# A new step order for a fused decoder: queries projected between the two halves of the weighing

## The reference

```python
for i in range(DEPTH):                                   # 6 layers
    x = attn_layer(shift_tokens(x), Wqkv[i], q_scale[i], k_scale[i], Wo[i]) + x
    x = ffn_layer(shift_tokens(x), ln_g[i], ln_b[i], W1[i], b1[i], W2[i], b2[i]) + x

def attn_layer(x, Wqkv, qs, ksc, Wo):                    # 16 heads of 64
    q, k, v = split(x @ Wqkv)                            # 128 -> 3 * 1024
    q = l2norm(q) * qs;  k = l2norm(k) * ksc
    q, k = rotary(q, k)                                  # x*cos + rotate_half(x)*sin, scaled
    sim = einsum(q, k_of_own_and_previous_window) * 8    # windows of 32, masked
    out = softmax(sim) @ v
    return out @ Wo                                      # 1024 -> 128

def ffn_layer(x, g, bln, W1, b1, W2, b2):
    xn = layernorm(x) * g + bln
    a, gate = split(xn @ W1 + b1)                        # 341 hidden, twice
    return a * gelu(gate) @ W2 + b2
```

## Time and profile before

| | |
|---|---|
| median of three runs | 2215.07 us |
| profiled execution, its own time | 2222.9 us |
| span of its trace | 2221.1 us |
| PE busy | 2012.4 us (91%) |
| DVE busy | 1410.5 us (64%) |
| ACT busy | 1384.2 us (62%) |
| POOL busy | 1090.0 us (49%) |
| mean granted TensorE clock | 0.983 of full speed |

### The profile page before, as it was taken

How to read it: one execution, slowest core, us unless ns; L and a number is a source line. 1 busy time by engine, 2 the same in 40 slices (tenths; PEclk the granted TensorE clock), 3 DMA queues, 4 the chain that set the end, 5 groups by cost and what they waited for, 6 DMA issues and landing times.

```text
span 2221.1 us, 74774 instructions
## 1 busy us (share of the span) xinstructions
PE 2012.4 (91%) x32616; PEld 1183.0 (53%) x32616; DVE 1410.5 (64%) x1975; ACT 1384.2 (62%) x2029; POOL 1090.0 (49%) x709
## 2 busy tenths in 40 slices
PE   8999997789998999999999999999899998999987
PEld 5655654355555555555555555555555555555553
DVE  1454444667766776676667667766677676667753
ACT  5555554466666666766666666666666666666664
POOL 0000000576665665565656656665556555556540
PEclk9999998799999999999999999999999999999998
DMA  3000000122223222232222323222322223222220
GB/s 106 1 1 1 1 20 29 39 59 59 59 68 78 68 69 59 64 93 62 68 62 68 85 58 84 61 58 69 78 69 69 59 59 88 67 69 59 60 59 20
DMA packets 82066, 128.11 MB, mean 58 GB/s; under 512 B 17230, under 2 KB 28108, under 8 KB 81740
## 3 DMA queue, kind: packets, MB, share of 16 engines
q1 hardware_dynamic: 81740, 123.33, 21.4%
HBM read 21.55 MB, written 1.05 MB: 10 GB/s over the span
## 4 chain that ended last, share of the span: by engine, by line
PE 66%; ACT 13%; issue 11%; DVE 7%; POOL 2%; DMA 0%; ACTq 0%; POOLq 0%; DVEq 0%; SPq 0%
PE ps L617 11%; PE ps L613 11%; PE ps L639 8%; PE ps L677 7%; PE ps L670 6%; PE ps L697 4%; PE ps L426 3%; PE ps L622 3%; DVE work L1104 2%; PE ps L626 2%; ACT work L974 2%; POOL work L1421 2%; ACT work L981 2%; DVE work L1252 2%; PE ps L519 1%
## 5 line engine op out<-in xcount | busy, mean ns | idle before, releaser
L1421 POOL TENSOR_TENSOR work<-work,RS 128x1024 f32<-128x1024 f32 x192 | 365.6, 1904 | 345.8 <-ACT RS L961 342.0
L617 PEld LDWEIGHTS ps<-ident,work 128*128 128x128 f32 x3072 | 344.4, 141 | 254.5 <-issue 112.9
L617 PE MATMUL ps<-ident,work 128*128 128x128 f32 x3072 | 408.7, 276 | 68.4 <-ACT work L981 32.0
L1099 DVE TENSOR_TENSOR work<-ps,work 128x512 f32<-128x512 f32 (+1 forms) x288 | 244.6, 849 | 253.7 <-ACT work L1019 182.5
L1442 POOL TENSOR_TENSOR work<-work 128x1024 f32<-128x1024 f32 x96 | 225.8, 2352 | 149.1 <-DVE work L1104 148.9
L1427 POOL TENSOR_TENSOR work<-work,RL 128x1024 f32<-128x1024 f32 x96 | 182.8, 1904 | 141.8 <-DVE RL L1159 141.8
L1432 POOL TENSOR_TENSOR work<-work 128x1024 f32<-128x1024 f32 x96 | 226.8, 2362 | 51.0 <-DVE work L1104 51.0
L1104 DVE TENSOR_TENSOR work<-ps,work 128x512 f32<-128x512 f32 (+1 forms) x288 | 246.9, 857 | 0.0
L1144 DVE TENSOR_REDUCE SS<-work 128x16 f32<-128x1024 f32 x192 | 231.9, 1208 | 0.0
L677 PEld LDWEIGHTS ps<-work 64*32 64x32 f32 x12288 | 136.2, 105 | 166.9 <-issue 153.8
L670 PEld LDWEIGHTS ps<-KT,work 64*32 64x32 f32 x12288 | 136.6, 105 | 127.5 <-issue 125.7
(11 more groups left out here) (184 smaller groups left out, 3177.9 us busy)
## 6 DMA issues: line engine op xcount, KB each, us to landing
work<-work SPq DMA_DIRECT2D x576, 128.0 KB
work<-work SPq DMA_DIRECT2D x336, 64.0 KB
WQ<-in_wqkv SPq DMA_DIRECT2D x6, 512.0 KB, 3.6
WK<-in_wqkv SPq DMA_DIRECT2D x6, 512.0 KB, 4.1
WV<-in_wqkv SPq DMA_DIRECT2D x6, 512.0 KB, 3.5
WO<-in_wo SPq DMA_DIRECT2D x6, 512.0 KB, 3.9
work<-ZR SPq DMA_DIRECT2D x48, 64.0 KB
W<-in_w SPq DMA_DIRECT2D x6, 341.0 KB, 3.0
```

The costliest lines, as they stand in the source:

```text
L617: m = nc.tensor.transpose(flat(R)[:, t * 128:t * 128 + 128], src[:, t * 128:t * 128 + 128], ident[:, :])
L1099: V.tensor_tensor(h16(cos_part[:, j, cols]), h16(src), rotary_tabs[:, at:at + 64].unsqueeze(1).broadcast_to([PARTS, heads_in, 64]), ALU.mu ...
L1421: U.tensor_tensor(h16(qk_norm[:, j, :]), h16(cos_part[:, j, :]), inv_norms[:, j, :].unsqueeze(2).broadcast_to([PARTS, 16, 64]), ALU.mult). ...
```

## The change

The same instructions are kept, and the order within a step is new on TensorE, ScalarE, VectorE and GpSimd; SyncE is the same.

- TensorE: the query projection of block g+1 now stands between `weigh(0, 4)` and `weigh(4, 8)` of step g (`queries`). The values come first in a step, then the turned heads, then the FFN or output piece, then the keys' turn. `variance` comes right behind the scores. In the second block's step the hidden chunks 0, 1 and 2 stand around the turns of the keys and the queries, and two thirds of `ffn_project` come before the weighing; its last third is in n = 2.
- ScalarE: `copy_heads` moves from the end of a step to the next one, behind the square of the queries. Exp of the scores moves from the start of the next step to the end of its own, ahead of `invert_norms(g, 1)`. In the second block's step the values are copied before the turned heads, the GELU table is loaded behind `copy_heads`, and the GELUs stand among the copies.
- VectorE: row sum and reciprocal move to the end of their own step; `norm` comes ahead of `sums(1)`; the three `gated` stand around the sin product and `sums(0)`.
- GpSimd: the order of the second block's `norm_product` is as in the other steps.

```diff
+            def queries(g):
+                pe.wait_ge(block_shifted, 2 * (g + 1))
+                pe.wait_ge(wq_loaded, 16 * (g // 16 + 1))
+                project(bank_z, w_q, 0, g % 4)
+                project(bank_z, w_q, 1, g % 4).then_inc(q_projected, 1)
...
-                if a:
...
-                    project(bank_z, w_q, 0, n)
-                    project(bank_z, w_q, 1, n).then_inc(q_projected, 1)
-                if d:
-                    pe.wait_ge(heads_copied, g - 2)
-                    turn(bank_y, heads).then_inc(heads_turned, 1)
                 if b:
                     pe.wait_ge(wv_loaded, 16 * ((g - 1) // 16 + 1))
...
+                if d:
+                    pe.wait_ge(heads_copied, g - 2)
+                    turn(bank_y, heads).then_inc(heads_turned, 1)
...
                 if f is not None and n == 2:
-                    ffn_project(f)
+                    ffn_project(f, 2, 3)
...
+                if f is not None and n == 1:
+                    pe.wait_ge(hidden_gated, 3 * f + 1)
+                    hid(1, bank_f)
                 if b:
                     if a:
                         pe.wait_ge(q_sin, g + 1)
                     pe.wait_ge(q_normed, g)
                     turn(bank_z, qk_norm[:, 0, :]).then_inc(q_turned, 1)
+                if f is not None and n == 1:
+                    pe.wait_ge(hidden_gated, 3 * f + 2)
+                    hid(2, bank_f)
...
+                if f is not None and n == 0:
+                    variance(f)
                 if f is not None and n == 1:
-                    pe.wait_ge(hidden_gated, 3 * f + 1)
-                    hid(1, bank_f)
+                    ffn_project(f, 0, 2)
...
+                if g + 1 < ALL_BLOCKS:
+                    if not b:
+                        pe.wait_ge(q_sin, g + 1)
+                    queries(g + 1)
                 if c:
                     weigh(4, 8).then_inc(heads_weighed, 1)
...
             def step(g, n, a, b, c, d, f, fo):        (ScalarE)
...
                     A(squares[:, 0, :], flat(bank_z), ACT.Square).then_inc(q_squared, 1)
+                if d:
+                    copy_heads(g - 1)
+                if f is not None and n == 1:
+                    nc.scalar.preload_act_table_set(GELU)
...
             def step(g, n, a, b, c, d, f, fo):        (VectorE)
...
                     rotary_cos(g, n, 0, flat(bank_z), slice(0, 1024), q_cos)
+                if f is not None and n == 1:
+                    gated(f, 0, bank_f)
+                if a:
...
                     rotary_sin(g, n, 0, flat(bank_z), slice(0, 1024), q_sin)
                     sums(0, g)
+                if f is not None and n == 1:
+                    gated(f, 1, bank_f)
+                    gated(f, 2, bank_f)
...
+                if f is not None and n == 0:
+                    norm(f)
                 if a:
                     sums(1, g)
-                if f is not None and n == 0:
-                    norm(f)
```

More of the change, by code:

```diff
@@ L751, in step @@
                     weigh(0, 4)
-                if f is not None and n == 0:
-                    variance(f)
-                if f is not None and n == 1:
-                    pe.wait_ge(gate_gelu, 3 * f + 2)
-                    hid_gate(2, bank_f)
                 if fo is not None and n == 2:
@@ L789, in finish @@
                 hid(2, bank_z)
-                ffn_project(f)
+                ffn_project(f, 0, 3)
                 last_centre(3)
@@ L795, in _ @@
             pe.wait_ge(ln_done, 8)
+            queries(0)
             for g in range(ALL_BLOCKS + 3):
@@ L999, in step @@
                 if f is not None and n == 1:
-                    nc.scalar.preload_act_table_set(GELU)
+                    gelu(f, 1, bank_f)
                 if b:
@@ L1150, in step @@
             def step(g, n, a, b, c, d, f, fo):
-                if f is not None and n == 2:
-                    gated(f, 2, bank_f)
-                if c:
-                    dve.wait_ge(probs_exp, g - 1)
-                    V.tensor_reduce(per_head(row_sum[:, :]), probs[:, :, :, :], AX, ALU.add).then_inc(probs_sum, 1)
-                    dve.wait_ge(probs_sum, g - 1)
-                    if due(g - 2):
-                        dve.wait_ge(probs_ready, g - 2)
-                    V.reciprocal(row_inv[:, :], row_sum[:, :]).then_inc(probs_inverse, 1)
                 if a:
@@ L1169, in step @@
                     sums(0, g)
+                if f is not None and n == 1:
+                    gated(f, 1, bank_f)
+                    gated(f, 2, bank_f)
                 if f is not None and n == 2:
                     update(f)
-                if f is not None and n == 1:
-                    gated(f, 0, bank_f)
                 if a:
@@ L1189, in step @@
                     V.tensor_tensor(scores_sb[:, :, :, :], by_head(bank_x), per_head(row_max[:, :]).unsqueeze(3).broadcast_to([PARTS, 8, 2, 64]), ALU.subtract).then_inc(scores_shifted, 1)
-                if f is not None and n == 1:
-                    gated(f, 1, bank_f)
+                if f is not None and n == 0:
+                    norm(f)
                 if a:
                     sums(1, g)
-                if f is not None and n == 0:
-                    norm(f)
+                if b:
+                    dve.wait_ge(probs_exp, g)
+                    V.tensor_reduce(per_head(row_sum[:, :]), probs[:, :, :, :], AX, ALU.add).then_inc(probs_sum, 1)
+                    dve.wait_ge(probs_sum, g)
+                    if due(g - 1):
+                        dve.wait_ge(probs_ready, g - 1)
+                    V.reciprocal(row_inv[:, :], row_sum[:, :]).then_inc(probs_inverse, 1)
                 if fo is not None and n == 3:
@@ L1436, in step @@
                         pool.wait_ge(block_shifted, 2 * g + 4)
-                    late = f is not None and n == 1
-                    if not late:
-                        norm_product(g, 0)
+                    norm_product(g, 0)
                     pool.wait_ge(k_cos, 2 * g + 2)
@@ L1443, in step @@
                     norm_product(g, 1)
-                    if late:
-                        norm_product(g, 0)
             def attention():
```

81 lines of the change are left out of this document (29 added, 52 removed).

## The result

| | before | after |
|---|---|---|
| median, same chip | 2215.64 us (2211.49 to 2217.62) | 2199.96 us (2197.05 to 2200.53) |
| ratio, 95% interval | | 0.9933 [0.992, 0.9946] |
| profiled execution, its span | 2222.9, 2221.1 us | 2197.05, 2195.3 us |
| mean granted TensorE clock | 0.983 | 0.987 |
| mean pass, blocks 8 to 88 | 73.59 us | 72.91 us |

A forecast was written before the change was run, and what follows sets the result against it. TensorE's queue, busy 91%, was taken as the bound. Per pass +5.65 - 2.9 + 0.2 - 0.8 = +2.15 us; 23 times that, +49 on 2222.9, gave about 2272, less 7.8 to the median: 2264 us, range 2216 to 2298.

The forecast's parts named there:

- The bound: TensorE's queue, busy for 91% of the span, is the line on which all gains and costs are added up.
- the waits removed: TensorE's waits for the turned heads' copy and for sin products (queries' and keys') can go: up to 2.9 us a pass.
- The new waits, +5.65: TensorE's new waits a pass: 4.6 us in the second block's step, 0.4 in n = 2, 0.65 in n = 0.
- The change from small to large matmuls, +0.2: On TensorE in n = 0, the queries add one change from small to large matmuls: 0.2 us a pass.
- "Issue", -0.8: TensorE stops in small matmuls: the long wait at the heads' turn swallows most of the weighing's, 0.8 us a pass.
- Fill and tail, 0 with 5 us either way: Passes 0 and 1 without an FFN, and the tail: no change, with 5 us either way.
- B: Faster: the chain of waits in n = 1 stays short, a pass gains 1.4 us, 2183 us; 13%.
- D: Slower still: TensorE's clock falls in the second block's step, 2303 us if every pass, 2284 if every second; 22%.
- A: Slower, 2264 us: the second block's step's waits outweigh those removed; own range 2229 to 2285; 60%.
- the two tests that I named: Heads' turn in n = 1 waiting under 1 us, or a pass under 73 us, would show the sum wrong.

The follow-up runs named there:

- four pairs: The kernel before and the changed kernel, both unmoved or with 16, 32 or 48 tiny matmuls ahead of the loop: after/before 0.9933, 0.998, 0.998, 0.996.
- queries_behind: Changed kernel with the queries' projection behind the second half of the weighing instead of between the halves: 2232.84 us, 1.0092.
- chunk_first: Changed kernel with hidden chunk 0 ahead of the heads' turn in n = 1 on TensorE: 2225.43 us, 1.0094.

## Why the prediction was wrong

**The bound, the waits removed and their places: right.** Both waits for the sin product went, and those for the copy of the turned heads came back in the new places that the forecast counts among the new waits. The three were 2.92 us a pass, as said.

**The new waits, +5.65: mis-sized, measured 4.07.** The moments at which they end were within 0.1 us. TensorE came to them later than I had it: at 6.54, 11.03, 12.63 and 16.63 us behind time 0 instead of 6.28, 10.9, 12.4 and 16.4. Two prices were low: the queries between small matmuls are 1.91 us from start to start, not 1.82; and ahead of a wait I took distances between starts (turn 0.88, half a chunk 0.86), where the last instruction runs to its end (1.06, 1.02). The idle time that a profile shows begins at that end. So my new waits were measured with a longer ruler than the 2.9 us removed, which I had read as idle times. In rows the four are 1.68 + 0.53 + 1.15 + 0.28 = 3.64 instead of 4.6; n = 2 is 0.39 (0.4), n = 0 0.39 (0.65). The mean is lower still, since L617's wait for `copy_heads` averages 1.39: stops in the weighing and the scores ahead take a part of it.

**The change from small to large matmuls, +0.2: not isolated, at most about that.** In the table above a pass without stops grew by 1.15 us, which is 4.07 - 2.92. By whole idle times it grew by 1.25, and TensorE's busy time per pass at full clock rose by 0.1 to 0.2 us in all four pairs (67.9 to 68.1 us unmoved). The overlap of two neighbours that each further wait breaks would do the same, and no run separates the two.

**"Issue", -0.8: the step that failed, measured -1.72.** I took the number of stops as given and let only the long wait swallow some, and so counted the weighing's alone (16.2 us). Swallowing is there, but it is worth 0.3 us a pass; most of the stops do not come at all. They fall where TensorE goes through many small instructions in a short time, and behind the start of a fetch, so I read them as TensorE running out of instructions. The new order puts large matmuls between the weighings and behind the scores, and 50 places are short instead of 79. For the weighing `queries_behind` shows this; for the scores, where the larger part was (26.5 to 8.4 us), no run isolates what did it. The rows had a warning: 27.3 us in the scores, which I left untouched, and the count of 258 in the earlier trace rows. The page "Runtime: NRT & Kernel Launch" of the Trainium skill, section "Instruction fetch mechanics", has the blocks of 256 instructions; its "mostly hidden" does not hold for runs of 64-column matmuls. I asked what that rule would make of the sum, and not which order brings the stops about. Why only 21 of 50 short places stop after the change, and 59 of 79 before, stays open.

With the measured terms the sum is 4.07 - 2.92 - 1.72 = -0.57. The point from which the change is slower lay not at 3.5 us of new waits but at 4.64, and 4.07 is below it. Each error alone would have changed the size; the two together turned the sign.

**Fill and tail, 0 with 5 us either way: too narrow.** In the four pairs the first eight blocks gained 3.6 to 8.9 us. No run tells why; the clock there differs too, with the smallest gain where it did not rise (0.927 before, 0.921 after) and the largest where it rose most (0.918 to 0.955).

**Rivals.** The result lies on B's side, 17 us from its 2183, but not by its mechanism: the heads' turn did wait 1.4 us in the mean and chunk 1 1.15. D occurred in part: in the five profiled executions of the changed kernel, moved or not, the clock fell behind the third wait of n = 1 in 2, 7, 4, 3 and 3 passes of some 22, each 1.1 to 1.7 us longer, where D's prices were for every pass or every second; `chunk_first` shows that the rule was one exchange away. A's range is also added up wrongly: 2264 with +18, -35 and 5 us either way is 2224 to 2287, not 2229 to 2285. The measured 2200 lies outside both. Of the two tests that I named, the heads' turn waited over 1 us, as forecast, and the pass was under 73 us: the sum was wrong.

## What to carry to other kernels

Add up what a new order idles with one ruler: durations to the end ahead of a wait, and idle times as the profile shows them, on both sides. Look for stops with nothing waited for in runs of small instructions, and put large ones between them: the new order as a whole has 1.7 us a pass less of them, nearly as much as the forecast's whole balance of 2.15. And before an order is judged by its waits, follow each back through the other engines: two instructions of `norm` in the wrong place, on no list of waits themselves, held 1.5 us a pass, and the order on ScalarE, with the `gated` exchange, another 2.1 (70.75 to 68.67 us, without stops at full clock).

## What the runs showed of the hardware that I had not expected

- TensorE can stop at every 256th instruction if the ones ahead are short (59 of 79 such places before the change, 21 of 50 after): 0.2 to 2.3 us, 2.1 to 2.4 us a pass before the change, and other matmuls are hit when 64, 128 or 192 instructions are put in ahead.
- Joining two waits into one of 2.25 us lowered the granted clock to its lower level behind it in 17 of 22 passes instead of 2: a ratio of 1.0094 instead of 0.9933, with 4 us less waiting between 700 and 2080 us. The same waits can be followed by either level: 1.69, 0.53 and 1.15 us left it at 1.00 in most passes and not in two.
- With 32 tiny matmuls ahead of the loop the ratio of the changed kernel went from 0.9933 to 1.0001. The clock alone does not explain it: the profiled execution had 17 us of the loop at the lower level instead of 7, but that of the unmoved kernel run again had 31, at a median ratio of 0.9941.
